# Summing the softmax probabilities of two heads in one GpSimd instruction (128x1024 instead of 128x512)

## What is computed

```python
# b = 8 batches, 512 queries and 512 keys, H = 16 heads of 32
score_prev = einsum('bhqd,bhkd->bhqk', q, k[:, :, :l1]) * SCALE    # masked by length
score_self = (q * k[:, :, l1:]).sum(-1, keepdims=True) * SCALE
weights = softmax(concat([score_prev, score_self], -1))
attn = einsum('bhqk,bhkd->bhqd', weights[..., :-1], v[:, :, :l1]) + weights[..., -1:] * v[:, :, l1:]
x = x + attn @ Wo + bo
x = x + concat([h @ W2 + b2, h @ We[idx] + be[idx]])               # h = gelu(x @ W1 + b1)
```

## Time and profile before

| | |
|---|---|
| median of three runs | 1747.89 us |
| profiled execution, device time | 1748.08 us |
| its span in the trace | 1745.8 us |
| outside the span | 2.3 us |
| PE busy | 1694.9 us, 97% of the span |
| DVE busy | 865.7 us, 50% |
| ACT busy | 703.5 us, 40% |
| POOL busy | 644.7 us, 37% |
| mean granted PE clock | 0.987 of full |

### The profile page before, as it was taken

One profiled execution on the slowest core, in us unless ns is written; L12 is line 12 of the kernel. 1 busy time (PEld: TensorE's weight loads), 2 busy tenths in 40 slices (PEclk: granted clock), 3 DMA queues, 4 the chain that ended last, 5 costly groups with the idle time before them and its releaser, 6 DMA issues.

```text
span 1745.8 us, 29761 instructions
## 1 busy us (share of the span) xinstructions
PE 1694.9 (97%) x9120; PEld 1285.4 (74%) x9120; DVE 865.7 (50%) x1370; ACT 703.5 (40%) x1223; POOL 644.7 (37%) x506
## 2 busy tenths in 40 slices
PE   5999999999999999999988799999999999999998
PEld 5766767667676666767655688888888888888886
DVE  4577575775757757577485433232322323232322
ACT  3254454543545535455344433233332323233321
POOL 3168494785857858567553001010000101010000
PEclk8999999999999999999988999999999999999999
DMA  6454554635546354553372514132231314132211
GB/s 138 84 124 101 114 110 100 133 93 115 111 106 127 89 118 106 119 120 92 89 167 78 181 56 85 56 55 80 38 83 48 85 48 89 54 62 78 38 23 24
DMA packets 392175, 157.90 MB, mean 90 GB/s; under 512 B 291666, under 2 KB 352082, under 8 KB 392098
## 3 DMA queue, kind: packets, MB, share of 16 engines
q1 hardware_dynamic: 360326, 144.00, 37.0%
q10 hardware_dynamic: 31772, 13.05, 2.9%
HBM read 77.75 MB, written 28.34 MB: 61 GB/s over the span
## 4 chain that ended last, share of the span: by engine, by line
PE 92%; DVE 3%; SPq 2%; DMA 1%; issue 1%; ACT 0%; POOL 0%; DVEq 0%; ACTq 0%
PE ps_proj L1388 20%; PE ps_score L1456 8%; PE ps_num L1469 7%; PE ps_max L1340 7%; PE ps_max L1341 7%; PE ps_max L1342 7%; PE ps_max L1429 6%; PE ps_proj L1410 5%; PE ps_score L1340 3%; PE ps_score L1342 3%; PE ps_score L1341 3%; PE ps_num L1341 3%; PE ps_num L1342 3%; PE ps_num L1340 3%; PE ps_max L1483 2%; PE ps_proj L1340 2%
## 5 line engine op out<-in xcount | busy, mean ns | idle before, releaser
L1037 DVE TENSOR_REDUCE m_col<-ps_max 128x1 f32<-128x512 f32 x512 | 333.1, 685 | 284.0 <-PE ps_max L1429 282.7
L813 ACT ACTIVATE p_f<-ps_score 128x512 f32<-128x512 f32 x512 | 306.1, 602 | 410.0 <-PE ps_score L1456 351.7
L681 POOL TENSOR_TENSOR p_sum<-p_sum,p_f 128x512 f32<-128x512 f32 x248 | 317.2, 1313 | 1.0 <-ACT p_f L813 1.0
L720 POOL TENSOR_TENSOR z_f<-z_f,a_raw 128x512 f32<-128x512 f32 x28 | 35.8, 1291 | 692.6 <-ACT z_f L926 669.9
L1241 DVE TENSOR_TENSOR h_lo<-h_f,h_hi 128x512 fp32r<-128x512 f32 x128 | 88.0, 688 | 404.1 <-ACT h_hi L917 403.9
L678 POOL TENSOR_TENSOR p_sum<-p_f 128x512 f32<-128x512 f32 x124 | 167.6, 1373 | 208.9 <-PE ps_max L1483 207.6
L1388 PE MATMUL ps_proj<-in_hi,w_hi 128*128 128x512 f32 x512 | 205.6, 402 | 14.5 <-POOL in_lo L686 7.3
L1456 PE MATMUL ps_score<-stacks 99*128 99x512 f32 x512 | 215.9, 424 | 3.1 <-ACT p_f L813 3.0
L1388 PE MATMUL ps_proj<-in_lo,w_hi 128*128 128x512 f32 x512 | 204.0, 398 | 0.0
L1388 PE MATMUL ps_proj<-in_hi,w_lo 128*128 128x512 f32 x512 | 203.8, 398 | 0.0
L1429 PE MATMUL ps_max<-stacks 97*128 97x512 f32 x512 | 182.8, 405 | 5.1 <-DVE m_col L1037 4.3
(11 more groups left out here) (144 smaller groups left out, 3016.3 us busy)
## 6 DMA issues: line engine op xcount, KB each, us to landing
stacks<-parts SPq DMA_DIRECT2D x384, 128.0 KB, 2.4
raw<-in_x_dram SPq DMA_DIRECT2D x128, 64.0 KB, 2.5
raw<-in_fside_BxSxS_dram SPq DMA_DIRECT2D x128, 64.0 KB, 2.8
spread<-own_scratch SPq DMA_DIRECT2D x128, 64.0 KB, 2.8
attn_scratch<-num SPq DMA_DIRECT2D x32, 256.0 KB, 3.0
we_raw<-in_L_cond_We_dram SPq DMA_DIRECT2D x32, 256.0 KB, 2.8
spread<-den_scratch ACTq DMA_DIRECT2D x124, 64.0 KB, 2.9
a_raw<-attn_scratch SPq DMA_DIRECT2D x30, 256.0 KB, 3.5
```

What stands on the lines that cost most here:

```text
L681: pool.tensor_tensor(p_sum[:, j], p_sum[:, j], p_f[:, i], ALU.add).then_inc(sum_made, 1)
L813: act.activation(p_f[:, i], ps_score[i % 2][:, :], ACT.Exp, scale=SCALE).then_inc(p_made, 1)
L1037: dve.tensor_reduce(m_col[:, n % C, n // C:n // C + 1], ps_max[n % 3][:, :], AX.X, ALU.max).then_inc(max_made, 1)
```

## The change

In `add_probabilities` one instruction adds both heads of a pair: `p_sum[:, j:j+2]` and `p_f[:, p:p+2]`, 128x1024 elements in place of 128x512. There are six additions a group. Their order on POOL is t = 1, 2, 3 for heads 0 and 1, then for heads 2 and 3, so each of t = 2 and t = 3 now waits for the addition just before it. The first needs both tiles of the pair. `sums_of` and `added` count the new way, and the four `in_lo` in the middle of group 1 stay between t = 2 and t = 3.

```diff
-    SUMS = HG * (C - 1)
+    SUMS = HG // 2 * (C - 1)
@@
         def sums_of(G, t, j):
-            return SUMS * G + 2 * (C - 1) * (j // 2) + 2 * (t - 1) + j % 2 + 1
+            return SUMS * G + (C - 1) * (j // 2) + t
 
         def added(n):
-            half, rest = divmod(n, 2 * (C - 1))
-            return 1 + rest // 2, 2 * half + rest % 2
+            half, rest = divmod(n, C - 1)
+            return 1 + rest, 2 * half
@@
                 G, (t, j) = C * b + g, added(n)
-                i = place_of(t, j)
-                pool.wait_ge(p_made, TILES * G + i + 1)
+                at, p0, p = slice(j, j + 2), place_of(0, j), place_of(t, j)
+                pool.wait_ge(p_made, TILES * G + p + 2)
                 if t == 1:
                     wait(pool, den_mm, G)
-                    pool.tensor_tensor(p_sum[:, j], p_f[:, place_of(0, j)], p_f[:, i], ALU.add).then_inc(sum_made, 1)
+                    pool.tensor_tensor(p_sum[:, at], p_f[:, p0:p0 + 2], p_f[:, p:p + 2], ALU.add).then_inc(sum_made, 1)
                 else:
                     pool.wait_ge(sum_made, sums_of(G, t - 1, j))
-                    pool.tensor_tensor(p_sum[:, j], p_sum[:, j], p_f[:, i], ALU.add).then_inc(sum_made, 1)
+                    pool.tensor_tensor(p_sum[:, at], p_sum[:, at], p_f[:, p:p + 2], ALU.add).then_inc(sum_made, 1)
@@
-                        if n == 4 and g == 1 and not last:
+                        if n == 2 and g == 1 and not last:
```

## The result

The changed kernel takes 1754.11 us (median of ten runs, 1751.49 to 1756.76), the kernel before 1747.80 in the same comparison (ten runs, 1746.37 to 1751.38). The ratio is 1.0034, with a 95% interval of 1.0024 to 1.0044: 0.34% or some 6 us slower, which is over the 0.2% that such a measurement can tell. The profiled run took 1754.63 us with a span of 1751.4, so 5.6 us more span than before.

What follows compares the result with a forecast made beforehand. The prediction took the attention loop to be bound by PE. To 1748.08 us it added 8.0 for the delayed copy in group 2 of seven batches and 0 for the last batch: 1756.1, so 1756, range 1745 to 1760.5.

Steps and rivals of the forecast that it cites:

- The pair: One POOL addition of 1024 columns takes 2.44 us (bounds 2.17 to 2.48); two of 512 take 2 x 1.293.
- The added wait: A POOL sum that waits for the one just before it starts 0.06 us after its end; upper bound 0.15.
- POOL in group 2: Four joined additions take 9.80 us where eight sums took 9.96, so POOL is 0.16 us earlier in group 2.
- DVE in group 2: The copy of the maxima waits out a joined addition, delaying PE's turn_max by 1.15 us in seven batches: 8.0 us.
- the copy slips in first: Rival, chance 0.34: joined addition under about 2.39 us, copy starts before it, PE loses nothing in group 2; 1749 us.
- Group 0 of batch 0: No term of its own; in groups 0 and 3 the copy was said to come before POOL starts.
- more than forecast: Rival, chance 0.09: late normalize in group 2 makes the maxima miss the next group's first tile; 1761 us.
- Groups 0 and 3 and their cover: normalize ends 1.15 us later there, the maxima reach SPq about 0.5 us later, hidden by some 2 us.
- The last batch: wide_low gets in sooner in group 2, PE's wait in group 3 grows by 2 to 3.5 us; together 0.
- The sum: Whole kernel: 1748.08 us now, plus 8.0 from group 2 of seven batches, plus 0 from the last batch: 1756.1 us.

Runs made afterwards that it cites:

- experiment 3: The kernel before, with its single sums ordered head by head so that each waits for the one before it: 1748.21 us, ratio 1.0000.
- experiment 4: The changed kernel with DVE's denominator moved ahead of the copy of the maxima, so that the copy comes behind POOL's first addition: 1792.11 us, ratio 1.0253.
- experiment 6: The changed kernel, where only in batch 0 the additions also wait for the copy of the maxima: 1748.78 us, ratio 0.9998.
- Experiment 2: The changed kernel, where the first addition of each half also waits until normalize is done: 1750.86 us, ratio 1.0014.
- experiment 1: The changed kernel, where the first addition of each half also waits for the copy of the maxima, in every group: 1748.58 us, ratio 1.0004.
- Experiment 8: The changed kernel with first additions waiting for the copy of the maxima, and the twelve sums of the last batch's group 2 single: 1744.65 us, ratio 0.9976.
- experiments 5 and 7: Both change the kernel before: 5 moves DVE's denominator ahead of the copy, ratio 1.0023; 7 makes the first sums wait for the copy, ratio 0.9986.

## Why the prediction was right, and where it wasn't

The forecast was 1756.0 us with 1745 to 1760.5; measured are 1754.11 (profiled 1754.63). The sign and the mechanism hold. The size is near by luck in part: the term of 8.0 us was to come from seven catches in group 2, and only two of them happened; the rest of the loss came from places that I had put at nothing.

**The pair: right, 0.05 us too long.** Forecast 2.44 us, measured 2.382 and 2.396 in the median, so the start that is saved is 0.19 to 0.20 us (2 x 1.293 - 2.39) and not 0.15. The two DVE rows gave a start that is 0.05 us small for POOL. By the straight line from the figure of the Trainium skill ("GPSIMD Engine Reference", section "3.1 Elementwise — side-by-side cycle accounting") the estimate was 2.36 us, 0.02 to 0.04 short of the trace where mine was 0.04 to 0.06 long.

**The added wait: right.** Two dependent pairs take 4.86 us, from start to end [after, 467.96], so their starts lie 4.86 - 2.40 = 2.46 us apart, 0.06 to 0.08 more than one takes. Forecast 0.06. Such waits cost nothing (experiment 3).

**POOL in group 2: 0.16 us forecast, 0.3 to 0.5 measured, and this decided.** Four pairs take 463.14 to 472.78 = 9.64 us, against 9.96 before and 9.80 forecast. `own_value` thus ends at 474.07, level with the denominators at 474.10; before it ended 0.43 us behind them (468.46 and 468.03). `q_lo` (L1015) waits for that end, and takes 1.20 us instead of 1.65; the copy comes 1.16 us after the denominators' start instead of 1.61. POOL's next sum starts 1.26 after it in both traces. I had the copy 0.19 us behind the pair (469.48 and 469.29); it was 0.10 ahead.

**DVE in group 2: the mechanism right, the count wrong.** This is the step that failed: "so 7 x 1.15 = 8.0 us". The size of a catch is right (1.07 and 1.12 us in batches 0 and 1, 1.04 to 1.30 in experiment 4; I had the copy end 0.12 us behind the sum, and it ends 0.07 behind). But it happened in two batches of the seven. In the trace before the copy came 0.42, 0.77 and 0.40 us behind the sum in batches 0 to 2 and 0.35 in the other four; after, it is 0.31 and 0.06 behind in batches 0 and 1 and 0.10 ahead in the rest. Why the first two differ was not worked out; in experiment 6 the catch of batch 1 stays when those of batch 0 are gone, so it is no sequel of them. In batches 2 to 6 the first rival, 'the copy slips in first', is what took place. It had named its own condition, a pair under 2.39 us, and the pair is at that bound to the hundredth. It was given 0.34 and would have been right on the loop: 0.57 us came off there. Its total of 1749 us was 5 us too low, for it too had nothing in group 0 of batch 0.

**Group 0 of batch 0: overlooked.** I wrote that in groups 0 and 3 the copy comes before POOL starts. That holds where the denominators release POOL. In group 0 of batch 0 there are none; the pair waits for its last exponential, and starts 0.2 us before the copy. The cost was 3.09 us: PE's wait is 1.54 us longer than before (1.90 and 0.36), and the rest, 1.55, is the lower clock behind it, which experiments 2 and 4 don't have after the same wait. The trace before showed the place: the longest of the three waits for L1044 in the earlier trace rows, 0.4 us, is this one. I read the row for its sum of 0.9 us and did not look where its three cases are.

**The sequel in batches 0 and 1: partly the rival 'more than forecast'.** In group 3 of batch 1 another 1.74 us went (0.46 in batch 0). The rows above suggest the way. ACT issues the transfers of the maxima in its own order; they wait for `m_parts`, which waits for `normalize`, and ACT's last exponential of the group comes behind them. It starts 1.32 us after `value_run` (259.92 and 258.60); before it started with it (both 254.21). The next score tile comes 4.37 us after the start of `value_run` instead of 3.57. The rival had SPq and the next group's first tile in mind; it was ACT. That this wait is the whole of the 1.74 is argued from one trace, not shown: experiment 6 has 1.35 there, and experiment 1, without the catch but with an equally long `normalize`, has -0.10. A late `normalize` costs only behind a copy that was already late.

**Groups 0 and 3 and their cover: right.** `normalize` takes 2.67 us in group 0 and 2.78 in group 3, forecast about 2.7. Experiment 2 takes the whole of that away and gains 0.13 us in five batches.

**The last batch: 0 forecast, +0.3 measured, from two large terms.** `wide_low` gets in sooner (-1.14 in group 2, -0.27 in group 1, bound -3.5), `attended_low` later: I put a turn at 2.9 us and it is 2.8, and PE's wait grows by 2.1 us (forecast 2 to 3.5). That leaves +1.70 in group 3. Together -1.4 + 1.7 = +0.3; experiment 1, with the same two waits, has +1.9, so that the two cancel is partly luck of the one trace. Experiment 8 shows that the two can be had apart.

**The sum.** Forecast +8.0 (all in group 2 of seven batches). In the trace: -1.4 of the start's spread, 3.1 + 1.1 + 0.5 in batch 0, 1.1 + 1.7 in batch 1, -0.6 in the loop, +0.3 in the last batch, which is 5.8. Without the start's spread it would be 7.3, and without the clock's 1.55 us in batch 0 as well 5.7; the medians say 6.3.

## What to carry to other kernels

- Of an instruction that blocks another engine's, the length is a price in itself. Joining two saves its start (0.2 us here) and doubles what a victim waits (1.29 to 2.38 us). Ask what each small instruction on that engine's critical path finds when it arrives, in the first and last rounds too, where other things release the work.
- Where two instructions start within 0.1 us of each other, as the copy and the pair do here, their order is more than a forecast can settle: mine was off by 0.29 us, from 0.19 behind to 0.10 ahead, and got it wrong in five batches of seven. If it matters, fix it by a wait: this one costs nothing that the runs show, and in the kernel before it gave 1.1 us of the trace in the first seven batches.

## What the runs showed of the hardware

- A copy of 128x112 within SBUF takes 0.22 us if it starts before the POOL sum of 2.38 and 2.1 to 2.4 us if it starts 0.05 to 0.3 us after it. Every value between in the traces is the rest of the POOL instruction under way. The Trainium skill ("SBUF — State Buffer", section "SBUF: two separate sides") has an exclusive lock for the whole instruction; these rows agree.
- DVE can be kept out over more than one POOL instruction: a `wide_low` that starts 0.08 us into a sum of 1.29 us takes 4.21, and 4.10 and 4.18 in experiments 5 and 7. That doesn't fit a lock of one instruction, and it doesn't happen beside every row of such sums (1.76 us in the earlier trace rows). Where each sum waits for the one before it, it took no more than the rest of the instruction under way (1.45 us in experiment 3, 2.70 with pairs).
- After PE had waited 1.90 us, its granted clock was 0.85 in the 2 us around that and 0.50 in the 2 us behind them, though PE was busy all through the latter. The same wait in experiments 2 and 4 left it at 1.00, and so did the waits of 0.97 us in experiment 4 and in batch 1. So the length of a wait alone does not say whether the clock falls.
